# Two-layer transformer block on Trainium2: values, gates and a running sum as fp32r products in two parts, and routed down products on 128 rows

## The reference, cut to what matters

```python
q, k = rope(hs @ Wq.T), rope(hs @ Wk.T)
v, g = hs @ Wv.T, hs @ Wg.T
s = clip(hs @ Ws1.T @ Ws2.T + bs2, -32, 32)
z = cumlogsumexp(s, axis=time); es = exp(s); enz = exp(-z)
ok = enz * (mask(q @ k.T * scale) @ es)
qv = softmax(ok)
o = mask((qv * enz) @ es.T) @ v
out = (o * rsqrt(mean(o * o) + eps) * g_norm * (g * sigmoid(g))) @ Wo.T
```

## Time and profile before

| | |
|---|---|
| median of 3 runs | 2058.89 us (2048.46 to 2060.23) |
| the profiled execution, its own time | 2074.86 us |
| its span in the trace | 2073.0 us |
| mean granted clock of TensorE in it | 0.977 |
| PE matmul busy | 1963.5 us, 95% |
| DVE, ACT, POOL busy | 1207.0, 820.1, 701.6 us (58%, 40%, 34%) |

### The profile page before, as it was taken

The page is one execution under the profiler, slowest core; times in us unless marked ns, Lnnn a source line. Parts: engine busy times, 40 slices in busy tenths (PEclk is TensorE's granted clock), DMA queues, the critical chain, the costliest instruction groups (busy, mean ns, idle before and its releaser), DMA issues.

```text
span 2073.0 us, 34692 instructions
## 1 busy us (share of the span) xinstructions
PE 1963.5 (95%) x12078; PEld 1517.9 (73%) x12078; DVE 1207.0 (58%) x2739; ACT 820.1 (40%) x2777; POOL 701.6 (34%) x790
## 2 busy tenths in 40 slices
PE   6999999999987999999999999999999998999976
PEld 4767666766665887888888888888888885666643
DVE  5776777753365576665565656655565563333366
ACT  3656454643332333334334343433434332333321
POOL 2000000310055443455555555555455551000064
PEclk9999999999998998999999999999999998999998
DMA  9500000123232000000000000000001223323233
GB/s 335 199 1 2 1 2 9 52 97 92 82 146 81 1 1 11 6 16 13 8 23 8 20 8 13 18 8 20 10 10 38 72 85 123 95 92 95 89 116 105
DMA packets 75897, 114.16 MB, mean 55 GB/s; under 512 B 9505, under 2 KB 65953, under 8 KB 73089
## 3 DMA queue, kind: packets, MB, share of 16 engines
q1 hardware_dynamic: 66416, 86.38, 12.5%
q0 software_dynamic: 9216, 25.18, 3.7%
q10 hardware_dynamic: 144, 1.05, 0.1%
HBM read 64.86 MB, written 47.71 MB: 54 GB/s over the span
## 4 chain that ended last, share of the span: by engine, by line
PE 83%; DVE 7%; issue 3%; POOL 2%; ACT 2%; DMA 1%; another core or an unknown queue 1%; DVEq 0%; SPq 0%; ACTq 0%; POOLq 0%
PE ps L1248 11%; PE ps L1239 10%; PE ps L1319 6%; PE ps L1632 5%; PE ps L583 4%; PE ps L1274 4%; PE ps L567 3%; PE ps L602 3%; PE ps L1262 3%; PE ps L1261 3%; PE ps L1260 3%; PE ps L1651 2%; PE ps L846 2%; PE ps L1255 2%; PE ps L573 2%
## 5 line engine op out<-in xcount | busy, mean ns | idle before, releaser
L1248 PE MATMUL ps<-weights,work 128*128 128x256 f32 x1024 | 268.6, 396 | 0.0
L1239 PE MATMUL ps<-work,weights 128*128 128x256 f32 x1024 | 244.4, 382 | 0.0
L1542 POOL TENSOR_TENSOR work<-work,rope 128x512 f32<-128x512 f32 x128 | 162.7, 1271 | 192.9 <-ACT work L1396 192.9
L1239 PEld LDWEIGHTS ps<-work,weights 128*128 128x128 f32 x1024 | 186.5, 192 | 21.5 <-DVE work L1452 0.8
L1248 PEld LDWEIGHTS ps<-weights,work 128*128 128x128 f32 x1024 | 183.4, 194 | 25.6
L1548 POOL TENSOR_TENSOR work<-work 128x512 f32<-128x512 f32 x128 | 162.0, 1265 | 5.1
L686 ACT ACTIVATE work<-ps,work 128x128 f32<-128x128 f32 x256 | 95.2, 372 | 150.7 <-DVE work L785 149.8
L445 POOL DMA_INDIRECT xg<-work x96 | 97.7, 1018 | 167.9 <-PE ps L573 155.9
L1827 POOL DMA_INDIRECT work<-yg,work x64 | 62.2, 971 | 271.4 <-DMA yg<-work 234.7
L1452 DVE TENSOR_TENSOR work<-ps,rope 128x512 f32<-128x512 f32 x128 | 87.9, 686 | 85.9 <-ACT work L1396 85.9
L724 DVE COPY work<-ps 128x384 f32<-128x384 f32 x256 | 129.6, 547 | 9.0 <-PE ps L583 8.9
(11 more groups left out here) (221 smaller groups left out, 4354.1 us busy)
## 6 DMA issues: line engine op xcount, KB each, us to landing
work<-xg SPq DMA_DIRECT2D x118, 128.0 KB
yg<-work SPq DMA_DIRECT2D x118, 128.0 KB, 1.7
xg<-work SPq DMA_DIRECT2D x6, 2048.0 KB, 17.0
weights<-in_w SPq DMA_DIRECT2D x8, 1024.0 KB, 10.5
weights<-in_f SPq DMA_DIRECT2D x8, 1024.0 KB, 4.9
weights<-in_f SPq DMA_DIRECT2D x1, 4864.0 KB, 17.2
work<-xn SPq DMA_DIRECT2D x32, 128.0 KB, 2.0
weights<-in_wo SPq DMA_DIRECT2D x1, 2048.0 KB, 8.8
```

The source lines that it names most:

```text
L1239: last = pe.matmul(ps[:, 2, which * SEQ:(which + 1) * SEQ], w1(h, (which * KC + kc) * P, P), xT[:, kc, :], start=kc == 0, stop=kc == KC - 1)
L1248: last = pe.matmul(ps[:, 3, c * 2 * DK:(c + 1) * 2 * DK], xT[:, kc, c * P:(c + 1) * P], w1(h, 2 * KC * DK + kc * 2 * DK, 2 * DK), start=kc ...
L1542: pool.tensor_tensor(qk[:, h % 4, :, :], raw[:, h % 2, :, :], rope[:, 0, :].unsqueeze(1).broadcast_to([P, 2, SEQ]), ALU.mult).then_inc(rot ...
```

## The change

1. `values_gates`: in place of fp32 products of 256 columns for one head and both halves of the tokens, it makes fp32r products of 512 columns for both heads of a pair and one half of the tokens (c = 0 or 1). Each is the sum of three terms, upper weights by upper x, lower weights by upper x, upper weights by lower x, over two chunks: 6 MATMULs, 12 for a pair. The upper parts of the weights are copied by ACT (`upper_vg`, two copies of 512 columns for each pair), the lower ones are made by POOL (`lower_vg`, even head) and DVE (`lower_vg`, odd head), one pair earlier than they are used. x is split once for each turn (`upper_x` on ACT, `lower_x` on DVE).
2. `running_sum`: two fp32 products become four fp32r ones. The upper part of `es` is a second exponential on ACT (256 columns), the lower part a subtraction on POOL (`lower_es`), which stands ahead of POOL's `rotate`.
3. The second down product of a routed block (both layers) reads all 128 rows, 64 of which are zero in h and in the weights.
4. `gates` on ACT and DVE take both heads for one half of the tokens in place of one head for both halves; sizes and counts stay. Buffers in SBUF are placed anew, and two small constants are made at the start.

```diff
             def running_sum(pp):
-                pe.wait_ge(es_ready.sem, es_ready.at(t, pp + 1))
-                pe.matmul(ps[:, 0, SEQ:2 * SEQ], keep_w[:, 0:P], es_both[:, pp % 2, 0:SEQ], start=True, stop=False,
-                          skip_group_check=True)
-                pe.matmul(ps[:, 0, SEQ + P:2 * SEQ], keep_w[:, P:2 * P], es_both[:, pp % 2, 0:P], start=False, stop=True,
-                          skip_group_check=True).then_inc(cum_done.sem, 1)
+                pe.wait_ge(es_lower.sem, es_lower.at(t, pp + 1))
+                for n in range(2):
+                    pe.matmul(ps[:, 0, SEQ:2 * SEQ], tri_r[:, :], es_split[:, n, :], start=n == 0, stop=False,
+                              skip_group_check=True)
+                for n in range(2):
+                    last = pe.matmul(ps[:, 0, SEQ + P:2 * SEQ], ones_r[:, :], es_split[:, n, 0:P], start=False, stop=n == 1,
+                                     skip_group_check=True)
+                last.then_inc(cum_done.sem, 1)
...
-                for c in tiles:
-                    for kc in range(KC):
-                        last = pe.matmul(ps[:, 3, c * 2 * DK:(c + 1) * 2 * DK], xT[:, kc, c * P:(c + 1) * P],
-                                         w1(h, 2 * KC * DK + kc * 2 * DK, 2 * DK), start=kc == 0, stop=kc == KC - 1)
...
+                if 0 in terms:
+                    if c == 0:
+                        pe.wait_ge(x1_lower.sem, x1_lower.at(t, n // PAIR1 + 1))
+                        pe.wait_ge(vg_lower_even.sem, vg_lower_even.at(t, n + 1))
+                        pe.wait_ge(vg_lower_odd.sem, vg_lower_odd.at(t, n + 1))
+                    if n or c:
+                        pe.wait_ge(gate_ready.sem, gate_ready.at(t, 2 * n + c))
+                for i in terms:
+                    (wp, xp), kc = TERMS[i // KC], i % KC
+                    last = pe.matmul(ps[:, 3, :], x1_split[:, xp, kc, c * P:(c + 1) * P], w_vg[:, n % 2, wp, kc, :],
+                                     start=i == 0, stop=i == KC * len(TERMS) - 1)
...
                 act.wait_ge(s_clipped.sem, s_clipped.at(t, pp + 1))
-                act.activation(es_both[:, pp % 2, :], s_clip, ACT.Exp).then_inc(es_ready.sem, 1)
+                act.activation(es_both[:, pp % 2, :], s_clip, ACT.Exp)
+                act.activation(es_split[:, 0, :], s_clip[:, 0:SEQ], ACT.Exp).then_inc(es_ready.sem, 1)
...
                 if ahead:
                     exp_scores(pp + 1)
                     copy_qk(2 * pp + 2)
+                if further:
+                    upper_vg(pp + 2)
...
                 if ahead:
-                    gates(2 * n)
+                    gates(n, 0)
+                if further:
+                    lower_vg(pp + 2)
+                if ahead:
                     rotate(2 * n + 1)
...
+                if part != "first" and pp == LAST - 1 and part != "last":
+                    lower_x(t + 1)
                 if ahead:
-                    gates(2 * n + 1)
+                    gates(n, 1)
...
+            def lower_es(pp):
+                pool.wait_ge(es_ready.sem, es_ready.at(t, pp + 1))
+                pool.tensor_tensor(es_split[:, 1, :], es_both[:, pp % 2, 0:SEQ], es_split[:, 0, :], ALU.subtract)\
+                    .then_inc(es_lower.sem, 1)
...
                 if ahead:
+                    lower_es(pp + 1)
                     rotate(2 * pp + 2)
...
                     rotate_end(2 * pp + 3)
+                if further:
+                    lower_vg(pp + 2)
...
-                pe.matmul(ps[:, 6 + b % 2, 0:D], h4T[0:64, b % 2, P:2 * P], experts1[0:64, bass.ds(offset[b] + (at + D), D)],
+                pe.matmul(ps[:, 6 + b % 2, 0:D], h4T[:, b % 2, P:2 * P], experts1[:, bass.ds(offset[b] + (at + D), D)],
                           start=False, stop=True).then_inc(y4_done.sem, 1)
```

More of the change, by code:

```diff
@@ L139, in build @@
         LEFT = (nc.sbuf_bytes_remaining // 4) - 8
+        SPLIT1 = 2 * KC * SEQ + 2 * 2 * KC * 4 * DK + 2 * SEQ
+        with nc.sbuf_tensor("split", [P, SPLIT1], F32R) as split:
+            pass
         work = sb("work", [P, LEFT])
@@ L145, in build @@
         room = {"attention": S_AT, "blocks": S_AT, "stay": S_AT, "slots": S_AT, "experts": S_AT, "route1": LEFT}
-        used = {"attention": 0, "blocks": 0, "stay": 0, "slots": 0, "experts": 0, "route1": S_AT}
+        used = {"attention": 0, "blocks": 0, "stay": 0, "slots": SPLIT1, "experts": 0, "route1": S_AT}
         def carve(loop, *shape, parts=P, dt=F32):
@@ L1196, in steps @@
             stays = part != "last"
-            return stays or pp < LAST, pp >= 0 and (stays or pp <= LAST), pp >= 1
+            return stays or pp < LAST - 1, stays or pp < LAST, pp >= 0 and (stays or pp <= LAST), pp >= 1
         def slots_over(eng):
@@ L1324, in pair @@
             def pair(pp):
-                ahead, now, behind = steps(pp, part)
+                further, ahead, now, behind = steps(pp, part)
                 if pp == LAST and ahead:
@@ L1391, in exp_scores, with upper_x, upper_vg @@
                 act.wait_ge(s_clipped.sem, s_clipped.at(t, pp + 1))
-                act.activation(es_both[:, pp % 2, :], s_clip, ACT.Exp).then_inc(es_ready.sem, 1)
+                act.activation(es_both[:, pp % 2, :], s_clip, ACT.Exp)
+                act.activation(es_split[:, 0, :], s_clip[:, 0:SEQ], ACT.Exp).then_inc(es_ready.sem, 1)
+            def upper_x(turn):
+                act.wait_ge(norm1.xT_ready.sem, norm1.xT_ready.at(turn, KC))
+                act.copy(x1_split[:, 0, :, :], norm1.xT).then_inc(x1_upper.sem, 1)
+            def upper_vg(n):
+                act.wait_ge(w1_loaded[n % PAIR1], 16)
+                for hh in range(2):
+                    act.copy(w_vg[:, n % 2, 0, :, hh * 2 * DK:(hh + 1) * 2 * DK],
+                             w1(2 * n + hh, 2 * KC * DK, 2 * KC * DK).rearrange("p (k w) -> p k w", k=KC))\
+                       .then_inc(vg_upper.sem, 1)
             def copy_qk(h):
@@ L1396, in copy_qk, with gates @@
                 act.copy(raw[:, h % 2, :, :].rearrange("p a b -> p (a b)"), ps[:, 2, :]).then_inc(raw_ready.sem, 1)
[L1398 to L1403, removed]
-                act.activation(gate[:, h % 4, :, :], vg[:, :, 1, :], ACT.Tanh, scale=0.5).then_inc(gate_tanh.sem, 1)
+            def gates(n, c):
+                act.wait_ge(vg_done.sem, vg_done.at(t, 2 * n + c + 1))
+                vg = ps[:, 3, :].rearrange("p (h w d) -> p h w d", h=2, w=2)
+                a = 2 * (n % 2)
+                act.copy(v1[:, a:a + 2, c, :], vg[:, :, 0, :]).then_inc(v1_ready.sem, 1)
+                if n >= 2 and c == 0:
+                    act.wait_ge(og_ready.sem, og_ready.at(t, n - 1))
+                act.activation(gate[:, a:a + 2, c, :], vg[:, :, 1, :], ACT.Tanh, scale=0.5).then_inc(gate_tanh.sem, 1)
             for pp in (-1, 0) if part == "first" else range(1, PAIR1 + 1):
-                ahead, now, behind = steps(pp, part)
+                further, ahead, now, behind = steps(pp, part)
                 if pp == LAST and ahead:
@@ L1472, in dve_slots @@
                 lower_s1(0, RANK_BANK)
+                lower_x(0)
+                lower_vg(0)
             def gated(pp):
```

73 lines of the change are left out of this document (52 added, 21 removed).

## The result

The changed kernel takes 1976.64 us (median of 4 runs, 1971.85 to 1979.21), the kernel before beside it 2058.43 us (2048.46 to 2060.23): ratio 0.961, 95% interval 0.957 to 0.965, faster by some 80 us. The forecast was 1972, with a range of 1944 to 2004. The profiled execution took 1976.93 us, of which its span is 1974.3.

The account below looks back on a forecast made before the run. PE was taken to bound the kernel: 2074.86 us, less 45 for 64 attention pairs, plus 2 at the start, less 43.7 for 118 routed blocks, gave 1988, and 16 less for the median 1972 us; range 1944 to 2004.

Parts of the forecast that it names:

- the two holes: Routed block: PE idle ahead of two weight loads where rows change between 128 and 64; 0.35 us a block, expected gone.
- the holes stay: Rival, routed blocks: holes belong to the down product, not the change of rows, and remain; 2016 us, chance 0.06.
- Values and gates: Attention pair on PE: 12 fp32r products stepping by 0.216 us take 2.59 us in place of 3.45, gain 0.86.
- Running sum: Attention pair on PE: four fp32r products take 0.43 us in place of 0.66, gain 0.23.
- The stand of `queries_keys` behind DVE's rotation: Attention pair: PE, arriving earlier, waits for DVE's rotation, whose end stays; 0.34 us lost, between 0.1 and 0.1 + 0.42.
- full 1.09: Rival, attention pair: POOL's rotation and L1508 don't meet, weight load hides, all 1.09 us gained; 1953 us, larger-gain chance 0.13.
- bound pair: Rival: pair soon bound by chain `slots_read`, DVE, L1239, or fp32r step 0.27; gains 0.3 us or less, 1998 us, chance 0.15.
- The 0.05 of `mix_values`: Attention pair: loss of 0.05 us at `mix_values`, whose DVE mask has as little time to spare.
- the pairs of the first turn in which DVE is late gain too: First attention turn: their chain runs through `slots_read` to `slots_write` on PE, so 0.70 us a pair counted there too.
- the full slowdown: Attention pair: DVE's L1508 meeting POOL's rotation takes 0.84 us in place of 0.42, so up to 0.42 us more.
- Start: Start of second attention: PE waits once for the first copies and subtractions; 2 us, bound 0 to 4.
- The 16 us taken off for the median: Whole kernel: profiled execution of 2074.86 us lay above the median of 2058.9, so 16 us less, 1988 to 1972.

Follow-up runs that it names:

- down_128: Kernel before with only the second down product of the routed blocks on 128 rows, both layers: 2014.72 us, ratio 0.982.
- down_96: Kernel before with the second down product of the routed blocks on rows 0 to 95: 2011.08 us in one execution.
- att_only: Changed kernel with the second down product back on 64 rows, so only the attention's part: 2017.03 us, ratio 0.982 to the kernel before.
- sum_fp32: Changed kernel with the running sum as two fp32 products again, without second exponential and `lower_es`: 1977.32 us in one execution.
- rotate_late: Changed kernel with one more wait, POOL's first rotation of a pair behind DVE's L1566: 1965.51 us, ratio 0.9555 to the kernel before.
- base_again: Kernel before, unchanged, profiled a second time: 2055.48 us in one execution.
- after_again: Changed kernel, unchanged, run once more: 1976.88 us, ratio 0.963 to the kernel before.
- vg_256: Changed kernel with each fp32r product of 512 columns in `values_gates` cut into two of 256: 1993.83 us in one execution.

## Why the prediction was right

**The blocks.** Right in mechanism and nearly in size: 2.49 us against 2.46, 0.344 a block against 0.37, 40.6 us against 43.7. The prediction's own working gave 2.48 us for a block and 0.35 for the two holes; it then took 2.46 and 0.37 without a reason, and the 3 us too many are this slip. down_128 and down_96 show that the holes belonged to the change to the 64-row form. The rival "the holes stay" (2016) is refuted.

**The steady pair.** 0.83 us against 0.70 forecast: two terms were mis-sized and nearly cancel.
- *Values and gates*: forecast 0.86, measured 0.65 (0.31 + 0.08 + 0.17 in the three groups, and 0.09 since the group behind L1318 starts earlier than its predecessor did behind L1290). The step of a fp32r product of 512 columns is not the 0.216 us taken from the fp32 row. In the group of six the first takes 0.32 and the others 1.48 - 0.32 = 5 x 0.233. Twelve times 0.017 is the missing 0.20. The bound of 0.27 was twice as far off on the other side.
- *Running sum*: forecast 0.23, measured 0.24, of which 0.16 lie in its own products and 0.08 in the transposes ahead of it.
- *The stand of `queries_keys` behind DVE's rotation*: forecast 0.34, measured 0.05, as DVE's chain stayed at 7.16 us and PE arrived 0.57 us earlier, 0.11 behind its end. The price was built from POOL's rotation slowing L1566. POOL's end did come to lie inside L1566, by 0.12 us, but at that overlap nothing is paid: L1566 ends 0.28 us behind POOL at the earliest, which is less than its own 0.42. The rival "full 1.09" failed for the first term, the "bound pair" for this one. (The first was also summed wrongly: 64 pairs of 1.09 are 70 us and not 64, so it stood for 1947 us.) That one term too high and one too low came out at nearly the same pair was luck. The 0.05 of `mix_values` did not show: a pair's parts leave nothing for it.

**The first turn.** This is the step that failed: "the pairs of the first turn in which DVE is late gain too". The forecast gave them 9 x 0.70 = 6.3 us; measured was +0.8 against the profile of before, and +4 to +7 against the other three traces with its attention. At equal clock it is less bad: with 0.94 the kernel before takes 163.7 us and att_only 161.2, with 0.96 down_128 takes 160.3 and sum_fp32 (without the new running sum) 158.1. So 2.2 to 2.5 of the 6.3 us came. Two things took the rest.
- *The meeting.* The argument left out that the chain through `slots_read` passes the very meeting of POOL and DVE that the earlier trace rows show. I priced the full slowdown at 0.42 us from that row, but a rotation that starts just ahead of DVE holds it for 0.98 us (1.40 - 0.42). The bound of that price should have been near POOL's whole duration (by the rule of the three durations 1.27 + 0.28 - 0.42 = 1.13). Steps 1 to 5, which the low clock reached in none of these four traces, show it alone: 78.4 us before, 78.4 changed, 75.5 with POOL moved behind L1566, 77.0 without `lower_es`. The meeting thus cost 2.9 us there, and 1.0 more in step 10. sum_fp32 and rotate_late, which move POOL's start to the one and the other side, show it as the cause: 4.7 us of waiting become 1.7 and 0.7.
- *The clock.* Steps 6 to 9 take 79.0 to 85.3 us in the four traces with the earlier attention and 82.6 to 86.1 in the changed kernel and att_only, and they follow the time at 1.2 GHz: from base_again to the first profile 13.7 us more of it go with 6.0 us more. The sum had no term for this. Whether the change itself lets the clock fall more often was not shown.

The later turns gave 42.4 us where 54 steps of 0.70 make 37.8. These 4.6 us more make up for a part of what the first turn lacked; that the total still came within 5 us is in part luck.

**Start and last stage.** +2.3 us for the start (forecast 2, bound 0 to 4), with 1.5 us of it a wait for L1515. The 16 us taken off for the median are confirmed by base_again.

**The sum by measured terms**: -42.4 for the later turns, about +1 to +7 for the first one, +2.3 for the start, +0.6 at the end, -40.6 for the blocks make -79 to -73, against 82 and 79 us measured between medians (the first comparison and that of after_again). The forecast of 87 us was thus 5 to 8 too high: at least 7 by the first turn and 3 by the blocks, less 4.6 by the later turns.

## What to carry to other kernels

A new instruction on an engine with idle time is not free by that: it moves every later start on its queue, and here 0.7 us of `lower_es` put POOL's rotation just ahead of a DVE instruction with two operands in SBUF. Look for the pairs that can meet, and take as the upper bound of a meeting's price nearly the whole POOL instruction, not the slowdown seen at another offset. A wait that keeps the two apart can give back more than the queue loses. Measure an edit's parts against each other, stage by stage: the running sum in fp32r parts gained 8 us in the steady turns, which one total of sum_fp32 would have called nothing. And compare a stage only at the same granted clock: of the 6.3 us by which the first turn then seemed to have lost, 4.9 lie where the clocks differ.

## What the runs showed of the hardware

- A fp32r product of 512 columns steps by 0.233 us when its load is hidden, the first of a group takes 0.32; one of 256 columns (vg_256) steps by 0.118, from single starts at 1163.42 and 1164.60 us with ten steps between them, and the first takes 0.20. So per 256 columns they cost 0.117 and 0.118, and width matters little. An fp32 product of 256 columns, two instructions, costs 0.43.
- A pair of changes between the 128-row and the 64-row form costs 0.34 us of PE; between 128 and 96 rows nothing (2.49 us for a block either way).
- L1566 on DVE (128x256, both operands in SBUF) takes 0.42 us alone, and ends 0.28 us behind POOL's 128x512 rotation where the two overlap by more than 0.14 us: 0.42, 0.84, 0.88 and 1.40 us at a start 1.18, 0.71, 0.69 and 0.18 us behind POOL's.
- With 12 more products a pair PE stood for about 2.7 us at each of the five jumps back of its loop, and each stand began as a packet of 16 KB started on its instruction queue; without them (1636 MATMULs and LDWEIGHTS a turn in place of 1828) the queue was still from 947 to 1569 us.
- In the first turn 13.7 us more at 1.2 GHz went with 6.0 us more of time (base_again and the first profile, the same kernel).
